# POOL's spread of the solved inverses goes one tile further ahead of the first product (two in place of one)

## The reference, cut to what matters

```python
k = x / max(norm(x), 1e-12)
v = (x @ W_write.T) * beta
A0 = tril(-(einsum('id,jd->ij', k * beta, k) * L), -1)
A = solve_triangular(eye - A0, eye, lower=True, unit_diagonal=True)
v = A @ v
attn = tril(einsum('id,jd->ij', k, k) * L)
o = attn @ v
return out + o @ W_read.T
```

## Time and profile before

| | |
|---|---|
| median of 3 runs | 874.53 us (874.52 to 875.96) |
| the profiled execution's own time | 880.48 us |
| its span, first to last instruction | 878.7 us |
| mean granted TensorE clock | 0.852 of 2.4 GHz |
| busy over the span: PE, DVE, POOL, ACT | 702.9, 450.1, 260.0, 228.7 us |

### The profile page before, as it was taken

How to read it: one execution, slowest core, us unless ns; L and a number is a source line. 1 busy time by engine, 2 the same in 40 slices (tenths; PEclk the granted TensorE clock), 3 DMA queues, 4 the chain that set the end, 5 groups by cost and what they waited for, 6 DMA issues and landing times. The chain is left out here.

```text
span 878.7 us, 13690 instructions
## 1 busy us (share of the span) xinstructions
PE 702.9 (80%) x4562; PEld 540.4 (62%) x4562; DVE 450.1 (51%) x1266; ACT 228.7 (26%) x635; POOL 260.0 (30%) x418
## 2 busy tenths in 40 slices
PE   5899999999963299999833774377459999999994
PEld 4567777676742189999722563366346666766673
DVE  2577777777754714447991658244633333333331
ACT  0233333333321334444310111011102222222221
POOL 2344444444420114544531211011010222222211
PEclk8899999999975579999965556556559999999998
DMA  8111111111000000000006500561510111111110
GB/s 320 56 33 33 33 33 33 32 33 33 2 1 1 2 1 7 6 7 24 7 3 210 240 1 1 148 238 31 220 51 19 55 47 45 54 55 48 44 42 19
DMA packets 24643, 49.77 MB, mean 57 GB/s; under 512 B 15284, under 2 KB 15414, under 8 KB 23936
## 3 DMA queue, kind: packets, MB, share of 16 engines
q1 hardware_dynamic: 20960, 34.43, 12.0%
q0 software_dynamic: 3328, 10.23, 3.9%
q10 hardware_dynamic: 288, 4.25, 1.2%
HBM read 39.03 MB, written 9.86 MB: 56 GB/s over the span
## 5 line engine op out<-in xcount | busy, mean ns | idle before, releaser
L1762 PE MATMUL psum<-arena_w,work 128*128 x208 | 96.7, 609 | 1.0 <-DVE work L1814 1.0
L1786 PE MATMUL psum<-arena_w,work 128*128 x416 | 94.2, 379 | 0.4 <-ACT work L1860 0.4
L1860 ACT ACTIVATE work<-psum,cst 128x128 f32<-128x128 f32 x208 | 56.5, 382 | 144.2 <-PE psum L1775 144.2
L1786 PEld LDWEIGHTS psum<-arena_w,work 128*128 128x128 f32 x416 | 77.1, 190 | 10.5 <-issue 1.1
L1130 PE MATMUL psum<-tokens,work 111*111 111x128 f32 x88 | 23.2, 410 | 64.1 <-POOL work L1537 64.1
L1724 POOL DMA_INDIRECT out<-work,row_i x26 | 25.7, 987 | 161.1 <-DVE work L1836 161.1
L1823 DVE COPY work<-psum 128x512 f32<-128x512 f32 x52 | 35.9, 691 | 70.9 <-PE psum L1762 61.7
L346 PE MATMUL psum<-arena_w 128*111 128x256 f32 x264 | 64.2, 396 | 4.8 <-DMA arena_w<-in_pack 4.8
L1762 PEld LDWEIGHTS psum<-arena_w,work 128*128 128x128 f32 x208 | 38.6, 196 | 40.4 <-issue 40.4
L711 POOL TENSOR_TENSOR arena_w<-arena_w,work 101x592 f32<-101x592 f32 x33 | 39.5, 1198 | 72.3 <-DVE work L577 72.3
L346 PEld LDWEIGHTS psum<-arena_w 128*111 128x111 f32 x264 | 46.7, 183 | 19.4 <-issue 9.5
(11 more groups left out here) (216 smaller groups left out, 1386.6 us busy)
## 6 DMA issues: line engine op xcount, KB each, us to landing
arena_w<-in_w SPq DMA_DIRECT2D x2, 4096.0 KB, 13.2
arena_w<-in_x SPq DMA_DIRECT2D x22, 333.0 KB, 2.9
x_rows<-tokens SPq DMA_DIRECT2D x22, 192.0 KB, 5.1
arena_w<-in_pack ACTq DMA_DIRECT2D x1, 2420.0 KB, 9.1
cst<-in_packc ACTq DMA_DIRECT2D x1, 1727.0 KB, 13.1
arena_w<-in_pack SPq DMA_DIRECT2D x1, 818.5 KB, 7.2
arena_w<-in_pack SPq DMA_DIRECT2D x2, 384.0 KB, 4.2
work<-a_rows SPq DMA_DIRECT2D x21, 32.4 KB, 2.0
```

The source lines that it names most:

```text
L1762: mm = nc.tensor.matmul(bank[2 * j + f][:, :], xgt[j][:, k * 128:(k + 1) * 128], arena_w1[:, bass.ds(expert * (2 * FF) + (k * FF + f * 512 ...
L1786: mm = nc.tensor.matmul(bank[7][:, 0:D], ht[j][:, g * 128:(g + 1) * 128], arena_w2[:, bass.ds(expert * (FC * D) + g * D, D)], start=(g == ...
L1860: nc.scalar.activation(ht[j][:, g * 128:(g + 1) * 128], bank[4 + f][:, k * 128:(k + 1) * 128], ACT.Gelu, bias=cst[:, bass.ds(expert * FC + ...
```

## The change

In POOL's tile loop the spread is called with t+2 in place of t+1, and the loop starts one step earlier, so that tile 0 is still spread first. `tile(t)` leaves out steps below 0 and above 21, so the number of spreads and powers stays 22 each. Before, POOL's order was spread(0), spread(1), power(0), spread(2), power(1), spread(3) and so on; after, it is spread(0), spread(1), spread(2), power(0), spread(3), power(1), spread(4). At the border of the groups spread(12) stood between power(10) and power(11); after, it stands between power(9) and power(10).

```diff
-                for t in range(-1, NT + 1):
+                for t in range(-2, NT + 1):
                     power_outputs(t - 1)
-                    spread_inverses(t + 1)
+                    spread_inverses(t + 2)
```

## The result

The median went from 875.05 us to 834.91 us, a ratio of 0.954 with a 95% interval of 0.952 to 0.956: 40.1 us less. The profiled execution took 836.92 us, with a span of 835.1 and a mean clock of 0.886 (before 0.852).

The account below looks back on a forecast made before the run. It took the second layer's attention loops to be bound by a ring through POOL's power and spread, with TensorE waiting. Shorter tile steps and starts save 33 us off the 874.53 us median, giving 841.5; range 830 to 850.

Parts of the forecast that it names:

- The likeliest case: Tile loops at 2.4 GHz for some three tenths of the time: 33 us saved, 841.5 us; chance 0.66.
- The ring and its end (step 1): Tile loops: solve, read-out, add_read, power, spread, solve takes 6.01 us; spread leaves the path, 31.1 us of waits go.
- The clock (step 3): Tile loops: denser TensorE gets 2.4 GHz more often; savings 25.7 us at 1.2 GHz, 45.3 at 2.4, 33 taken.
- The first rival: Tile loops: clock holds at 2.4 GHz once TensorE is dense, 45.3 us saved, 829 us; chance 0.18.
- step 2: Tile loops: DVE is the next limit, about 4.05 us a tile early, 3.17 in the last ten, below TensorE's 4.70.
- The border (step 4): Between groups: normalise(10) waits behind spread(12), cost 0 under about 1.9 us of cover; substitution ends equally far behind tile 11.
- the second wait (step 5): POOL's spread(t+2) also needs solve(t) done, since there are two blocks; cost 0.
- Signs that were named and did not come: TensorE's spread waits fall to about 33 us in 2 waits; middle stretch 21 to 23; tile step not under 3.2.
- The loops did not stay at 1.2 GHz: Rival for the tile loops: clock gains nothing or falls to 1.2 GHz throughout, 25.7 us saved, 848.8 us; chance 0.09.
- the substitution didn't keep the first group's gain: Rival: substitution on DVE bounds the first group, only the last ten tiles gain, 15.8 us, so 859; chance 0.03.
- no other wait held the spread in the loops: Rival: block free or inverses landed holds the spread, so it comes no earlier, 874.5 us; chance 0.02.
- the expert stage: Rival: this stage stays long at 1.2 GHz; 80 us there gives 881.5 us, slower; chance 0.02.

Follow-up runs that it names:

- The filled kernel before: Kernel before the change, with three unused idle products behind the router product in nearly every step; 859.43 us, ratio 0.981.
- the run with add_read first: Changed kernel with DVE's add_read(t-1) put ahead of normalise_outputs(t-2) in each tile step; 831.49 us, ratio 0.949 to before.
- the 42 idle products: Changed kernel with 42 unused products on TensorE behind tile 11, during the wait for the second group's inverses; 836.30 us, ratio 0.955 to before.
- three blocks: Changed kernel with three blocks in place of two for spread inverses, each spread a further tile ahead from tile 15 on; 835.96 us, ratio 0.954 to before.
- both edits of DVE: Changed kernel with substitution budget 3.4 in place of 1.7 and add_read ahead of normalise; 826.14 us, ratio 0.942 to before.

## Why the prediction was right, and where it wasn't

The time, 834.9, lies in the range of 830 to 850, and the direction was right. The likeliest case was not what happened: 841.5 was 6.6 us too high, and the saving of 33 was 40.1.

- **The ring and its end (step 1) held.** The waits for the spread fell from 31.1 to 7.0 us inside the loops. Nothing new came on ACT's side. At 1.2 GHz the step is TensorE's own, as said, 4.53 us where 4.70 was worked out; the next solve starts while the router product's record is still open.
- **The clock (step 3) was mis-sized, and this is the term that was off.** "I take 33 ... 0.3 rather than today's 0.2": the share of time at 2.4 GHz was taken as three tenths. The clocks of 0.82 and 0.80 make it (0.82 - 0.5)/0.5 = 0.64 and 0.60. Put 0.62 in the prediction's own formula, and the steps are 1/(0.38/4.70 + 0.62/4.05) = 4.27 and 1/(0.38/4.70 + 0.62/3.17) = 3.61, saving 15.4 + 20.2 + 3.8 = 39.4 us. That this meets the 40.1 of the medians is partly luck: the formula works on the profiled executions, and between these the span fell by 43.6 us. Stretch by stretch it gives too little: 19.2 of 21.1 us in the first group with its start and border, 20.2 of the 22.1 that the nine steps of the last ten tiles gained (52.7 to 30.5 from solve to solve). Only for the last ten is a higher share of 2.4 GHz the reason; for the first group see below. The row that was taken to speak against a high share, TensorE busy from 310 us on at 0.50, is no lasting state. The five us ahead of it have 0.75 with TensorE busy 3.34 us, the five behind it 0.73, and then comes

```profile
320.00:325.00 5.00, 5.00 (x26) 4.15 (x25) 2.73 (x8) 1.31 (x3) 0.62 (x1) 1.00 0.00 0
```

In the changed kernel too TensorE was busy at 1.2 GHz for its first 12 us behind the border and then went to 2.4. The filled kernel before shows what the clock gives in the old order, 18.1 us.
- **The first rival was nearly the case.** The clock didn't hold throughout: each group begins at 1.2 GHz (three steps of about 4.5 us behind the border), and in the profiled execution it fell once in the first group. Where it did hold, DVE's ring was the limit at 3.08 us against the 3.17 worked out (step 2), and the run with add_read first shows that it was the ring with POOL's power in it. By the Trainium skill, "TensorE: Matmul & The Clock Gate", section "What's actually happening", activity releases the throttle. The traces agree in part: 0.60 becomes 0.82 and 0.95 as the gaps close or are filled, but behind the border TensorE was busy for about 12 us before it was granted 2.4 GHz.
- **DVE as the first group's limit (steps 2 and 4) was seen only in part.** The prediction had "at the lower clock DVE costs nothing" and took the first group's saving from TensorE's steps, weighted by the clock. It was 21.1 us from the first spread to spread(12) (88.3 to 67.2), the upper end of the 15 to 21 that its steps and start made, and it was the same with the clock at 0.82 and at 0.89. What is saved is DVE's idle time of 19.7 us. In the changed kernel DVE has none left and its steps set the pace (from 482.68 to 517.44 us nine add_reads come 3.86 us apart in the mean, where about 4.05 was worked out), TensorE runs ahead, and so the border grew by 3.3 us where "21 to 23" was forecast. The substitution's last steps did not "fall at the same distance behind tile 11". A kernel with the old order and more substitution per tile saves 16.5 us.
- **The border (step 4) and the second wait (step 5) cost nothing**, as said. The slack ahead of add_read(11) is 1.81 us where about 1.9 was forecast. The one trace of step 5 is a wait of 0.97 us of POOL for the first solve, at the start, long before it matters.
- **The other rivals fell.** The loops did not stay at 1.2 GHz, the substitution didn't keep the first group's gain, no other wait held the spread in the loops, and the expert stage took 222.2 us as before.
- **Signs that were named and did not come.** TensorE's waits for the spread fell to 43.4 us in 11 waits, not to about 33 in 2. Steps of 2.57 us are well under the "not under 3.2 anywhere": TensorE takes them at 2.4 GHz until DVE holds it back, which the prediction left out.

What stays open: what decides when TensorE is granted 2.4 GHz behind the border. What the low stretch costs is 1.2 to 1.5 us a step by the traces, and the medians show no gain clear of their scatter.

## What to carry to other kernels

When a wait goes that made TensorE idle for a fifth of each step, ask what its clock will do, and price both ends: here the filling of the gaps alone, in the old order, gave 18 us where the new order gave 40. Then ask stage by stage whether TensorE sets the pace at all: a higher clock in the changed kernel's first group (0.89 for 0.82) made it no shorter. An engine that looks half idle can still be the bound of a stage, if it has a fixed amount of work to finish before a border; add up its idle time over the whole stage, since that is the most that a shorter step can give back. And the order of two instructions on a third engine (power, spread) can tie two loops together that have no data between them; the same held for DVE's normalise ahead of add_read.

## What the runs showed that was not expected

- The level was lost in two steps behind a pause of 1.8 us that followed 23.6 us of dense products. The changed kernel's first group had waits of 0.6 to 1.5 us in five of its steps, with a clock of 0.82 and one fall. Its second profiled execution had eight such waits (0.4 to 1.5 us), with 0.89 and no fall.
- Behind the border TensorE ran at 1.2 GHz with no idle time at all from 540.63 on and was granted 2.4 GHz only about 12 us later (the solve at 553.81 is the first short one). This delay is not fixed. The first short solve came 13.2 us behind the first one in both profiled executions of the changed kernel, about 9 with the 42 idle products and with three blocks, and 4.1 with both edits of DVE.
- The doubled substitution budget shortened the changed kernel as well, by moving two tiles' work of DVE into a wait for DRAM.
